# A Mamba and FP4 layer on one core: replicated loads by unit of 32 channels over all partitions

## The chip, the cores and the metric

The kernel runs on one core of a Trainium2 chip. The metric is the device time of one execution in microseconds (us). TensorE multiplies matrices, VectorE, ScalarE and GpSimd work elementwise, SyncE only issues DMAs and waits; 16 DMA engines move data between HBM (DRAM) and the 128 partitions of on-chip memory.

## The reference

The input `x` has 4 sequences of 2048 tokens with 256 features, 8192 tokens in all. It is normalised, goes through four Mamba layers with a residual, and then through a gated feed-forward block whose activations and weights are quantised to FP4 in blocks of 16. The part around the change is the selective scan of each Mamba layer: 512 channels `d`, 16 states `n`:

```
dA = exp(delta[t, d] * A[d, n])
h  = h * dA + (delta[t, d] * u[t, d]) * B[t, n]
y[t, d] = sum over n of h * C[t, n]   (+ u * D_skip, then * silu(z), then the output projection)
```

Each of the 512 x 16 pairs (channel, state) is a recurrence over the tokens of its sequence; `delta` and `delta*u` do not depend on the state, `B` and `C` do not depend on the channel.

## The kernel before

The program has three blocks one after another: `normalise_input`, `mamba_layers` and `fp4_ffn`. The change is in `mamba_layers`. That works through 64 chunks: 4 layers times 16 chunks of T = 512 tokens (four chunks make a sequence). A chunk is a turn of 16 groups (`s` = 0 to 15). A group is one set of 4 states (`j = s % 4`) of one block of 128 channels (`q = s // 4`), and its rows are laid out so: partition 32*k + r holds state 4*j + k of channel 32*unit + r, and the free dimension holds unit 0 to 3 and 512 tokens. So 4 units of 32 channels make the 128 channels, and 4 states stand side by side over the partitions.

For this layout three things have to be copied to each of the four groups of 32 partitions:

- `drep[q % 2]` (128 x 4 x 512): delta of block q, once per k. ScalarE reads it in `exp` (L603) to make `dA`, one group ahead of the scan.
- `durep[q % 2]` (same size): delta*x. VectorE multiplies it with `B_all` in `times_b` (L935) to make `bu`; then `scan` (L950) makes `h`.
- `crep[:, j, :]` (128 x 4 x 512): C of state 4*j + k on partitions 32*k to 32*k + 31. GpSimd multiplies it with `h` in `times_c` (L832).

The sources are three DRAM scratch tensors: `delta_dram` and `du_dram` (512 channels x 512 tokens, stored from `za` by `store_delta` and from `relu` by `store_du`) and `c_dram` (16 states x 512 tokens). They are written and read back in each chunk; both have two halves for alternate chunks. All these DMAs are issued by SyncE, in the order in which `turn` is written, and each may wait for a semaphore first. In turn g the order is: C unit 3 and durep block 1 of this chunk; the stores and loads of x; drep 2, durep 2; the store of the next chunk's C; drep 3, durep 3; the next x; then for the next chunk the stores of delta (`store_delta`, L372) and of delta*x (`store_du`, L376), drep 0, durep 0, C units 0 and 1, drep 1, C unit 2. drep and durep have two buffers each, so the load of block q + 2 waits until all of block q has been read; crep has one buffer per j and waits until the last group of the chunk before has been multiplied.

Before, `replicate` (L348) fills one buffer with four DMAs, one per k: DMA k writes partitions 32*k to 32*k + 31 with all four units, and its source pattern is 32 rows, 4 units, 512 floats. `load_c` (L342) fills crep for one j with four DMAs: each writes 32 partitions with the same row. Each buffer has its own semaphore; a DMA adds 16 when it has landed, so a consumer waits for 64 per load. VectorE waits for durep in front of the first `times_b` of a block, ScalarE for drep in front of the first `exp`, GpSimd for crep in the first four groups of a chunk.

GpSimd also computes delta (`za`) and delta*x (`relu`, L854) for the next chunk during the groups 7 to 11 of this one. The turns run in a hardware loop of four chunks per pass (`turns`).

Of the kernel before, what the change touches and what calls it, by code (L numbers as in the profile page):

```python
# [11 lines left out]
P = 128  # L12
T = 512
# [11 lines left out]
def positive(count):  # L25

    return not isinstance(count, int) or count > 0
# [88 lines left out]
def mamba_layers(nc, xbuf, w, NL, L, sem, x_stored):  # L116
# [17 lines left out]
    with ExitStack() as ctx:  # L134
        def sb(name, shape, dt=F32):
            return ctx.enter_context(nc.sbuf_tensor(name, shape, dt))
# [32 lines left out]
        crep = sb("crep", [P, QS, T])  # L169
# [8 lines left out]
        c_dram = nc.dram_tensor("c_dram", (2, 4 * QS, T), F32, kind="Internal").ap()  # L178
# [12 lines left out]
        c_loaded = [sem(f"c_loaded{j}") for j in range(QS)]  # L191
# [93 lines left out]
        def _(sp):  # L285
# [50 lines left out]
            def load_c(n, p_, j):  # L336
                if positive(n):
                    sp.wait_ge(hc_ready, 2 * (NG * (n - 1) + NG - QS + j) + 2)
                if j == 0:
                    sp.wait_ge(c_stored, 16 * (n + 1))  # L340
                for k in range(4):
                    sp.dma_start(crep[32 * k:32 * k + 32, j, :],  # L342
                                 c_dram[p_, 4 * j + k].partition_broadcast(32)).then_inc(c_loaded[j], 16)

            def replicate(dst, src, q, done):
                rows = src[P * q:P * q + P].rearrange("(g r) t -> r g t", r=32)
                for k in range(4):
                    sp.dma_start(dst[32 * k:32 * k + 32], rows).then_inc(done, 16)  # L348

            def load_delta(n, p_, q):  # L350

                if q >= 2:
                    sp.wait_ge(da_ready, 4 * NG * n + 16 * (q - 2) + 16)
                elif q == 0:
                    sp.wait_ge(delta_stored, 16 * (n + 1))
                elif positive(n):
                    sp.wait_ge(da_ready, 4 * NG * n)
                replicate(drep[q % 2], delta_dram[p_], q, d_loaded[q % 2])

            def load_du(n, p_, q):  # L360

                if q >= 2:
                    sp.wait_ge(bu_ready, 2 * NG * n + 8 * (q - 2) + 8)
                elif q == 0:
                    sp.wait_ge(du_stored, 16 * (n + 1))
                elif positive(n):
                    sp.wait_ge(bu_ready, 2 * NG * n)
                replicate(durep[q % 2], du_dram[p_], q, du_loaded[q % 2])
# [28 lines left out]
            for j in range(QS):  # L397
                load_c(0, 0, j)
# [7 lines left out]
            def turn(g, ph):  # L406
                n, p_ = g + 1, 1 - ph % 2
                if not is_first(g):
                    load_c(g, 1 - p_, 3)
                load_du(g, 1 - p_, 1)  # L410
                if not is_first(g):
                    at_layer(g, ph, lambda layer: load_skip(layer, g))
                    if not (isinstance(g, int) and g == 1):
                        store_x(g - 2)
                    load_res(g - 1, (ph - 1) % 4)
                load_delta(g, 1 - p_, 2)
                load_du(g, 1 - p_, 2)
                if not is_last(g):
                    store_c(n, p_)
                load_delta(g, 1 - p_, 3)  # L420
                load_du(g, 1 - p_, 3)
                if not is_last(g):
                    if not (isinstance(g, int) and g == TOT - 2):
                        at_layer(g + 2, (ph + 2) % 4, lambda layer: load_inw(layer, g + 2))
                        at_layer(g + 2, (ph + 2) % 4, load_mid)
                        load_x(g + 3)
                    store_delta(n, p_)
                    store_du(n, p_)
                    load_delta(n, p_, 0)
                    load_du(n, p_, 0)  # L430
                    load_c(n, p_, 0)
                    load_c(n, p_, 1)
                    load_delta(n, p_, 1)
                    load_c(n, p_, 2)
# [384 lines left out]
        def _(pool):  # L819

            def times_c(at):
                n, s, G = at
                j = s % QS
                if s < QS:
                    pool.wait_ge(c_loaded[j], 64 * (n + 1))
                r = 4 * (s % 2)
                for k in range(2):
                    pool.wait_ge(scanned, 4 * G + 2 * k + 2)
                    if positive(2 * G + k - 3):
                        pool.wait_ge(summed, 2 * G + k - 3)  # L830
                    pair = slice(r + 2 * k, r + 2 * k + 2)
                    pool.tensor_tensor(hc[:, pair, :], h[:, pair, :], crep[:, j:j + 1, :].to_broadcast([P, 2, T]),  # L832
                                       ALU.mult).then_inc(hc_ready, 1)
# [57 lines left out]
            def turn(g, ph):  # L891
                other = 1 - ph % 2
                for s in range(NG):
                    if not is_last(g):
                        if s == 2:
                            silu_xc(g + 1, other)
                        if s == 7:
                            softplus(g + 1, other, 0)
                    times_c(group(g, s))
                    if not is_first(g):  # L900
                        if s == 10:
                            variance(g - 1)
                        if s == 12:
                            newton_step(g - 1)
                    if not is_last(g):
                        if s == 8:
                            softplus(g + 1, other, 1)
                        if s in (10, 11):
                            softplus(g + 1, other, s - 8)
                    if not is_first(g):  # L910
                        if s == 15:
                            affine(g - 1, 0)
                            affine(g - 1, 1)
# [721 lines left out]
```

## Time and profile before

| | |
|---|---|
| time of 3 runs | 8876.08, 8876.52, 8879.55 us; median 8876.52 |
| the profiled execution | 8879.16 us, span in the trace 8877.4 us |
| VectorE busy | 8002.6 us (90%) |
| GpSimd busy | 6905.2 us (78%) |
| TensorE busy | 6565.6 us (74%) |
| ScalarE busy | 5352.6 us (60%) |
| DMA | 910 MB, 42% of the 16 engines' time |

Engines are named PE (TensorE), PEld (its weight loads), DVE (VectorE), ACT (ScalarE), POOL (GpSimd) and SP (SyncE; SPq is its sequencer, which issues the DMAs). L348 is line 348 of the kernel. Times are microseconds from the span's start unless marked ns. Releasers (after `<-`) are inferred from semaphore events.

### The profile page before, as it was taken

The numbers are of one execution on the slowest core, as the hardware profiler recorded it, in microseconds if no ns is written. First come the engines' busy times: TensorE is split into PE (matmuls) and PEld (weight loads), VectorE is DVE, ScalarE is ACT, GpSimd is POOL, SyncE is SP. The second block draws the span as 40 slices with busy tenths as digits, with TensorE's granted clock in tenths as the row PEclk, the third lists the DMA queues.
The fourth block names the chain that finished last, engine by engine and source line by source line (L and its number), as shares of the span: only waits on it lengthen the run. The fifth ranks groups of instructions, "written<-read, shape, count | busy, mean of one in ns | idle before, by whom it ended". The sixth has DMA issues, their size and how long they took to land. (4 is left out here: it accounts for less than half of the span.)

```text
span 8877.4 us, 97211 instructions
## 1 busy us (share of the span) xinstructions
PE 6565.6 (74%) x21284; PEld 2595.9 (29%) x21284; DVE 8002.6 (90%) x8268; ACT 5352.6 (60%) x8662; POOL 6905.2 (78%) x3198
## 2 busy tenths in 40 slices
PE   3777777778777777777777777777777777646656
PEld 1222222222222222222222222222222222224434
DVE  3999999999999999999999999999999999845555
ACT  2666666666666666666666666666666666422222
POOL 1888888888888888888888889888888889732222
PEclk9899998989899999898899989898989999767888
DMA  4444454544444544454445545444445455310000
GB/s 136 105 105 112 115 119 110 119 122 113 106 110 113 119 111 118 112 128 115 99 113 117 119 110 119 122 113 106 110 113 119 112 117 119 71 36 22 24 26 24
DMA packets 568694, 910.48 MB, mean 103 GB/s; under 512 B 58320, under 2 KB 203088, under 8 KB 566992
## 3 DMA queue, kind: packets, MB, share of 16 engines
q1 hardware_dynamic: 568016, 903.29, 42.4%
q8 instruction: 200, 3.28, 0.2%
q14 instruction: 478, 3.92, 0.2%
HBM read 716.41 MB, written 186.65 MB: 102 GB/s over the span
## 5 line engine op out<-in xcount | busy, mean ns | idle before, releaser
L832 POOL TENSOR_TENSOR hc<-h,crep 128x1024 f32<-128x1024 f32 x2048 | 4785.0, 2361 | 834.8 <-PE acc L473 748.6
L950 DVE TENSOR_TENSOR_SCAN h<-dA,carry,bu 128x512 f32<-128x512 f32 x3072 | 3768.2, 1265 | 92.7 <-ACT dA L603 46.7
L935 DVE TENSOR_TENSOR bu<-durep,B_all 128x1024 f32<-128x1024 f32 x2048 | 2483.2, 1212 | 194.6 <-DMA durep<-du_dram 146.1
L603 ACT ACTIVATE dA<-drep,cur 128x512 f32<-128x512 f32 x4096 | 2618.6, 710 | 14.5 <-DMA drep<-delta_dram 14.5
L455 PE MATMUL B_all<-dtc,spread_b 128*128 128x512 f32 x2048 | 1360.6, 752 | 1638.1 <-DVE bu L935 1636.6
L612 ACT COPY carry<-h 128x4 f32<-128x4 f32 x1023 | 200.9, 196 | 2223.5 <-DVE h L950 2168.7
L473 PE MATMUL acc<-hc,gather 128*32 128x512 f32 x8192 | 1281.8, 702 | 5.5 <-POOL hc L832 5.5
L950 DVE TENSOR_TENSOR_SCAN h<-dA,bu 128x512 f32<-128x512 f32 x1024 | 1196.7, 1206 | 9.9 <-ACT dA L603 7.8
L493 PE MATMUL work<-xT,inw 128*128 128x512 f32 x2048 | 1020.6, 644 | 60.5 <-ACT xT L623 50.0
L455 PEld LDWEIGHTS B_all<-dtc,spread_b 128*128 128x128 f32 x2048 | 367.6, 213 | 2321.5 <-DVE bu L935 2258.2
L503 PE MATMUL work<-xs,taps 128*128 128x512 f32 x2048 | 964.1, 614 | 0.0
L493 PEld LDWEIGHTS work<-xT,inw 128*128 128x128 f32 x2048 | 400.5, 207 | 758.9 <-issue 662.1
L1073 POOL TENSOR_TENSOR f_f_qh_xn<-f_hid,f_f_qh_rec 128x704 f32<-128x704 f32 x64 | 101.5, 1585 | 630.7 <-DVE f_f_qh_rec L1068 630.7
L503 PEld LDWEIGHTS work<-xs,taps 128*128 128x128 f32 x2048 | 376.1, 194 | 617.9 <-issue 617.9
L1280 PE MATMUL f_down<-f_wdT,f_hqT 128*128 128x256 f32 (+1 forms) x768 | 259.7, 494 | 341.1 <-ACT f_hqT L1329 341.1
L531 PE MATMUL work<-outw,sz 128*128 128x256 f32 x2048 | 489.6, 382 | 0.0
L473 PEld LDWEIGHTS acc<-hc,gather 128*32 128x32 f32 x8192 | 173.0, 116 | 979.8 <-issue 688.0
L844 POOL TENSOR_TENSOR quad<-quad,xs 128x2048 f32<-128x2048 f32 x64 | 289.4, 4522 | 160.2 <-ACT quad L701 160.2
L531 PEld LDWEIGHTS work<-outw,sz 128*128 128x128 f32 x2048 | 394.4, 193 | 55.6
L837 POOL TENSOR_TENSOR xc<-xc,quad 128x2048 f32<-128x2048 f32 x64 | 289.9, 4530 | 142.0 <-ACT quad L668 142.0
L462 PE MATMUL acc<-xc,skip 128*128 128x512 f32 x512 | 339.4, 752 | 0.0
L1280 PEld LDWEIGHTS f_down<-f_wdT,f_hqT 128*128 128x128 f32 (+1 forms) x768 | 177.4, 246 | 413.1 <-ACT f_hqT L1329 358.6
(167 smaller groups left out, 7151.8 us busy)
## 6 DMA issues: line engine op xcount, KB each, us to landing
drep<-delta_dram SPq DMA_DIRECT2D x1024, 256.0 KB, 6.0
durep<-du_dram SPq DMA_DIRECT2D x1024, 256.0 KB, 6.7
crep<-c_dram SPq DMA_DIRECT2D x1024, 64.0 KB, 6.5
delta_dram<-za SPq DMA_DIRECT2D x64, 1024.0 KB, 4.3
du_dram<-relu SPq DMA_DIRECT2D x64, 1024.0 KB, 5.3
x_in<-xbuf SPq DMA_DIRECT2D x65, 512.0 KB, 3.8
x_res<-xbuf SPq DMA_DIRECT2D x64, 512.0 KB, 3.9
xbuf<-x_res SPq DMA_DIRECT2D x64, 512.0 KB, 5.6
```

What stands on the lines that cost most here:

```text
L455: pe.matmul(B_all[:], spread_b[:, s % QS, :], dtc[:, p_, :], start=True, stop=True).then_inc(bb_ready, 1)
L462: pe.matmul(acc[:], skip[:, q, :], xc[:, p_, q, :], start=True, stop=False, skip_group_check=True)
L473: ins = pe.matmul(acc[32 * k:32 * k + 32, :], gather[:], hc[:, 4 * (s % 2) + k, :], start=False, stop=s % QS == QS - 1, skip_group_check=True)
L493: ins = pe.matmul(W[b][:], inw[:, k, z * DI + e * P:z * DI + (e + 1) * P], xT[:, k, :], start=k == 0, stop=k == KD - 1)
L503: ins = pe.matmul(W[b][:], taps[:, 4 * e + k, :], xs[:, e, k:k + T], start=k == 0, stop=k == 3)
L531: ins = pe.matmul(half, sz[:, p_, k, t * P:(t + 1) * P], outw[:, k, :], start=False, stop=k == DB - 1)
L603: act.activation(dA[:, 4 * (s % 2) + k, :], drep[q % 2][:, k, :], ACT.Exp, scale=cur[:, p_, 4 * s + k:4 * s + k + 1]).then_inc(da_ready, 1)
L832: pool.tensor_tensor(hc[:, pair, :], h[:, pair, :], crep[:, j:j + 1, :].to_broadcast([P, 2, T]), ALU.mult).then_inc(hc_ready, 1)
L837: pool.tensor_tensor(xc[:, p_], xc[:, p_], quad[:], ALU.mult).then_inc(xc_ready, 1)
L935: dve.tensor_tensor(bu[:, 2 * k:2 * k + 2, :], durep[q % 2][:, 2 * k:2 * k + 2, :], B_all[:].unsqueeze(1).to_broadcast([P, 2, T]), ALU.mul ...
L950: dve.tensor_tensor_scan(h[:, r, :], dA[:, r, :], bu[:, k, :], start, ALU.mult, ALU.add).then_inc(scanned, 1)
L1280: ins = pe.matmul(down[:, 0:D], hqT[0:rows, tt % 2, k, :], wdT[0:rows, k, :], start=k == 0, stop=k == GT - 1)
```

## The change

`load_c` and `replicate` are cut the other way. A DMA of `replicate` now takes one unit of 32 channels and writes it to all 128 partitions, that is four times; its source is the 32 rows with a leading level of 4 and step 0. `load_c` takes the four states of one j in one DMA: the source is 4 rows, each repeated 32 times through a step of 0 in the middle. The number of DMAs for drep and durep stays four per block; for C it goes from four to one per j, and GpSimd waits for 16 instead of 64. What stands where in the buffers is the same.

```diff
@@ -338,14 +338,12 @@
                     sp.wait_ge(hc_ready, 2 * (NG * (n - 1) + NG - QS + j) + 2)
                 if j == 0:
                     sp.wait_ge(c_stored, 16 * (n + 1))
-                for k in range(4):
-                    sp.dma_start(crep[32 * k:32 * k + 32, j, :],
-                                 c_dram[p_, 4 * j + k].partition_broadcast(32)).then_inc(c_loaded[j], 16)
+                sp.dma_start(crep[:, j, :], c_dram[p_, 4 * j:4 * j + 4].unsqueeze(1).to_broadcast([4, 32, T])).then_inc(c_loaded[j], 16)
 
             def replicate(dst, src, q, done):
-                rows = src[P * q:P * q + P].rearrange("(g r) t -> r g t", r=32)
-                for k in range(4):
-                    sp.dma_start(dst[32 * k:32 * k + 32], rows).then_inc(done, 16)
+                for unit in range(4):
+                    rows = src[P * q + 32 * unit:P * q + 32 * unit + 32]
+                    sp.dma_start(dst[:, unit, :], rows.unsqueeze(0).to_broadcast([4, 32, T])).then_inc(done, 16)
 
             def load_delta(n, p_, q):
 
@@ -822,7 +820,7 @@
                 n, s, G = at
                 j = s % QS
                 if s < QS:
-                    pool.wait_ge(c_loaded[j], 64 * (n + 1))
+                    pool.wait_ge(c_loaded[j], 16 * (n + 1))
                 r = 4 * (s % 2)
                 for k in range(2):
                     pool.wait_ge(scanned, 4 * G + 2 * k + 2)
```

## Rows read from the trace of the kernel before

**Rows 1.** The page: busy time of each engine, and VectorE's slices.
```profile
PE 6565.6 (74%) x21284; PEld 2595.9 (29%) x21284; DVE 8002.6 (90%) x8268; ACT 5352.6 (60%) x8662; POOL 6905.2 (78%) x3198
DVE  3999999999999999999999999999999999845555
```

**Rows 2.** Waits of VectorE: us in total, times, longest us.
```profile
DVE bu L935 <- DMA durep<-du_dram: 146.1, 38, 99.1
```

**Rows 3.** The page's DMA issues: count, KB each, median us to landing.
```profile
drep<-delta_dram SPq DMA_DIRECT2D x1024, 256.0 KB, 6.0
durep<-du_dram SPq DMA_DIRECT2D x1024, 256.0 KB, 6.7
```

**Rows 4.** Windows: busy us per engine, clock, DMA share, GB/s.
```profile
4070.50:4071.50 1.00, 1.00 (x10) 0.16 (x9) 1.00 (x2) 0.00 (x0) 1.00 (x2) 1.00 1.03 389
4079.50:4080.50 1.00, 1.00 (x4) 0.40 (x3) 1.00 (x2) 0.31 (x2) 1.00 (x2) 1.00 1.01 379
4004.50:4012.00 7.50, 5.63 (x19) 1.89 (x18) 6.96 (x7) 3.39 (x7) 6.60 (x4) 1.00 1.06 210
4034.00:4039.00 5.00, 1.76 (x10) 0.16 (x8) 4.57 (x5) 5.00 (x9) 3.00 (x2) 1.00 1.07 220
4085.00:4091.00 6.00, 5.90 (x23) 1.97 (x26) 6.00 (x7) 3.83 (x8) 6.00 (x4) 1.00 1.06 214
212.00:7740.00 7528.00, 5831.65 (x18746) 2125.39 (x18750) 7329.88 (x6899) 5029.16 (x8062) 6555.18 (x2988) 0.90 0.48 113
```

**Rows 5.** Timeline of SyncE at a chunk boundary: start, us, what, count.
```profile
4077.84 0.36 SPq L376 DMA_DIRECT2D du_dram<-relu  x1
4078.32 3.20 SPq L348 DMA_DIRECT2D drep<-delta_dram  x4
4083.09 1.73 SPq L348 DMA_DIRECT2D durep<-du_dram  x4
4085.01 5.68 SPq L342 DMA_DIRECT2D crep<-c_dram  x8
4090.80 1.78 SPq L348 DMA_DIRECT2D drep<-delta_dram  x4
4093.04 7.72 SPq L342 DMA_DIRECT2D crep<-c_dram  x8
```

**Rows 6.** Timeline: GpSimd's delta*x, VectorE's first product of blocks 0 to 3.
```profile
4073.25 4.56 POOL L854 TENSOR_TENSOR relu<-za,xc 128x2048 f32<-128x2048 f32 x1
...
4094.15 1.23 DVE L935 TENSOR_TENSOR bu<-durep,B_all 128x1024 f32<-128x1024 f32 x1 [2.11 <-DMA durep<-du_dram]
...
4122.91 1.23 DVE L935 TENSOR_TENSOR bu<-durep,B_all 128x1024 f32<-128x1024 f32 x1 [0.31 <-PE B_all L455]
...
4151.36 1.21 DVE L935 TENSOR_TENSOR bu<-durep,B_all 128x1024 f32<-128x1024 f32 x1
...
4181.36 1.23 DVE L935 TENSOR_TENSOR bu<-durep,B_all 128x1024 f32<-128x1024 f32 x1
```

**Rows 7.** The C loads of line 342: ns min/median/max of one issue.
```profile
L342 SPq DMA_DIRECT2D crep<-c_dram x1024: 302/421/1878, 155.0 to 7635.3; - x171
```

**Rows 8.** Timeline of ScalarE and VectorE where the four-chunk loop turns.
```profile
4209.78 1.21 DVE L935 TENSOR_TENSOR bu<-durep,B_all 128x1024 f32<-128x1024 f32 x1
...
4215.19 0.20 ACT L612 COPY carry<-h 128x4 f32<-128x4 f32 x1 [6.62 <-issue]
...
4218.63 1.28 DVE L950 TENSOR_TENSOR_SCAN h<-dA,carry,bu 128x512 f32<-128x512 f32 x1 [6.47 <-ACT dA L603]
...
4245.61 1.23 DVE L935 TENSOR_TENSOR bu<-durep,B_all 128x1024 f32<-128x1024 f32 x1 [0.49 <-PE B_all L455]
```

**Rows 9.** Timeline of the very start of the Mamba part.
```profile
190.13 3.64 SPq L348 DMA_DIRECT2D drep<-delta_dram  x8
...
193.81 0.43 SPq L376 DMA_DIRECT2D du_dram<-relu  x1
...
204.50 1.73 SPq L348 DMA_DIRECT2D durep<-du_dram  x4
...
211.34 1.23 DVE L935 TENSOR_TENSOR bu<-durep,B_all 128x1024 f32<-128x1024 f32 x1 [99.11 <-DMA durep<-du_dram]
```

## The prediction

> **What bounds the kernel now.** I read the page's busy shares and slices first [rows 1], then who waits for whom on VectorE [rows 2], then the DMA issues and the rate of the transfers by stretch [rows 3, 4], and last the order of time at one chunk boundary [rows 5, 6]. The page says that VectorE is busy in over 90% of nearly every slice up to the 33rd, where the Mamba part ends; in the stretch from 212 to 7740 us it works 7330 of 7528 us [rows 4]. GpSimd is behind it with 6555 us. So the 64 chunks follow VectorE, at about 117.7 us each (first product of the first chunk at 211.3 us, of the one read here at 4094.2, 33 chunks later [rows 6, 9]).
>
> VectorE's only sizeable wait on a transfer is 146.1 us for durep, in 38 places, 99.1 of it at the very start [rows 2]; the other 47 us are 0.75 us per chunk boundary. That small number is the important one: it says that the first durep load of a chunk lands just when it is needed, with no reserve. The chain at a boundary [rows 5, 6]: GpSimd finishes delta*x at 4077.8 us, SyncE stores it, issues drep for block 0 behind it (4078.3), durep for block 0 at 4083.1, and VectorE starts the chunk at 4094.2 after 2.1 us of waiting.
>
> **The rates.** I call "a block" the four DMAs that fill one drep or durep buffer: 4 x 256 KB = 1.05 MB [rows 3]. In stretches that hold only such loads the 16 DMA engines are all busy (share 1.06) and move 210, 220 and 214 GB/s; in stretches that hold only a store of all 128 partitions they are as busy (1.03, 1.01) and move 389 and 379 GB/s [rows 4]. So an engine moves 24.0 GB/s when it writes or reads alone and 13.4 GB/s in the replicating loads. Those write 32 partitions per DMA with 16 engines; the factor 1.8 says that the way into 32 partitions carries eight engines' worth. A block now takes b = 1.05 MB / 214 = 4.9 us.
>
> **The change, part by part.**
>
> Issues. The C load goes from 16 to 4 issues per chunk, 768 fewer in all, at 0.42 us each [rows 7]: 323 us of SyncE, which computes nothing and mostly waits in this kernel. At the boundary the C loads stand behind the first durep in SyncE's order [rows 5], so nothing on the path moves forward: I take 0. The ends are -323 us, if every issue stood on the path, and, since a three-level issue has no row of its own, 2304 issues times the 1.46 us between the median and the longest one, which SyncE's idle time would mostly hide; both ends are far from the nearest row, a SyncE that waits between the blocks [rows 5]. The wait for one completion instead of four costs nothing. drep and durep keep their four issues per block; their bytes, and their places in the buffers, stay too.
>
> Shape. Each new DMA writes all 128 partitions, which takes the factor 1.8 away if all 16 engines work on it. But its source is now a three-level pattern: 4 copies with step 0, then 32 rows, then 512 floats. The destination is 128 rows. No transfer in the trace has an outermost level below 16, and none shows how such a one is dealt out. Two ends: all 16 engines, 384 GB/s, b = 2.7 us; or, if the engines get equal shares of the outermost level, four shares on four engines. Four at 24.0 GB/s give 96 GB/s and b = 10.9 us; four at the slower 13.4 give 53.6 and b = 19.6 us. The second slows again because engine 0 would fill partitions 0 to 31 while engine 1 fills 32 to 63, and so on; if such neighbours meet on the same way into the memory as the engines of a 32-partition DMA do today, each gets half. I take four engines: dealing out the outermost level is what fits every full-rate row (128 or 32 rows over 16 engines), and a level of 4 can't be cut further. Between 10.9 and 19.6 I take b = 12.0: only two engines meet on eight ways, not sixteen, and they meet only when both are at the same four-or-so rows, so I allow a tenth.
>
> The Trainium skill, page "DMA: Bandwidth & Descriptors", section "Why a DMA increments its semaphore by 16 and not by 1", says that the number of engines is the largest up to 16 that divides the slowest non-1 dimension of both patterns, and its rules for kernel authors name a leading zero-stride broadcast of c copies as confined to at most c engines; by this rule b lies at 10.9 or above, and no run so far shows it. The page "SBUF — State Buffer", section "Door 1: The DMA port swizzle", speaks against the neighbours: partitions p and p+32 are on the same port, and 64 partitions reach no more ports than 32. The 214 against 384 GB/s agrees with it; by it alone four engines in step would be at 19.6.
>
> Where b falls on the path, per chunk (a C load is b/4, in the same queue):
>
> 1. Chunk start. From delta*x ready to durep landed are now 16.3 us: the store (1.05 MB / 384 = 2.7), drep (4.9), durep (4.9), and 3.8 of issue and landing. It becomes 16.3 + 2(b - 4.9). As the reserve is nil, all of it is stall: 14.2 us at b = 12.0. Nothing earlier can hide it: drep block 0 waits for the delta store, but is issued after the delta*x store in SyncE's order. What is queued behind VectorE's wait is every scan.
>
> 2. Block 1. After the first durep, in order: C units 0 and 1, drep 1, C units 2 and 3, durep 1: b/4 x 4 + 2b = 3b after the start of the chunk. VectorE asks for durep 1 after block 0: 28.8 us in the chunk of [rows 6] (4094.15 to 4122.91), and 35.8 us (4209.78 to 4245.61) in every fourth chunk, where ScalarE stands still 6.6 us at the edge of the four-chunk loop and VectorE behind it [rows 8]; that is 49 and 14 chunks. 3b is 14.7 now and hidden; at b = 12.0 it is 36.0: a stall of 7.2 us in 49 chunks and 0.2 in 14.
>
> 3. Blocks 2 and 3. The x stores and loads come first (3 us), then 2b = 24.0: 27.0 against the 28.4 that block 1 takes (4122.91 to 4151.36 [rows 6]): hidden, with little over. Block 3 has 24.0 against 30.0 (to 4181.36): hidden.
>
> 4. The very start. drep 0, drep 1 and durep 0 stand in a row before the first product [rows 9]: 3(b - 4.9) = 21 us.
>
> Sum at b = 12.0: 63 x 14.2 + 49 x 7.2 + 14 x 0.2 + 21 = 895 + 353 + 3 + 21 = 1272 us. On the profiled execution (span 8877.4, its own time 8879.2, which is 2.7 above the median of 8876.5) that is a span of 10,149; the median follows at **10,150 us**. By the same steps b = 10.9 gives 756 + 191 + 18 = 965, about 9,840. b = 13.5 gives 1084 + 573 + 66 + 26, and block 2 then asks 30.0 where 28.4 are to be had, 1.6 x 63 = 101: 1,850, about 10,730. The FP4 part behind 7790 us has none of these loads and stays.
>
> **The rivals.**
>
> A. The neighbours share fully, b towards 19.6. For it: the same engines do get half today [rows 4]. Against: today eight ways are loaded by sixteen engines at all times, there two engines walk over eight ways. Price at b = 19.6: start 63 x 29.4 = 1852; block 1 (58.8 - 28.8) x 49 + 23 x 14 = 1792; block 2 (3 + 39.2 - 28.4) x 63 = 869; block 3 (39.2 - 30) x 63 = 580; 44 at the very start: 5137, so 14,010 us. In that case the four engines are the bound (9 blocks x 19.6 = 176 us per chunk and the stores beside it). Half way, b = 15: 1273 + 794 + 129 + 290 + 30 = 2516, 11,390 us.
>
> B. All 16 engines are used, b = 2.7, and the kernel is faster. What decides it is the dealing out alone, at any count of engines that gives b below 4.9 (nine or more at 24 GB/s). It takes away the 47 us at the boundaries and 3 x 2.2 at the start: 8,823 us. For it: destination rows are 128, as in the fast stores; more than that is not to be had, since VectorE's own work is 97% of the stretch. Against: the zero-step level of 4 on the outside.
>
> C. Four engines, but the stall is hidden by something I take for serial, no change within 0.2% (18 us, about what a measurement of this kernel can tell from nothing). Against: the 0.75 us of wait per boundary leaves no reserve for even one block.
>
> **How the numbers follow.** Four engines with b from 10.9 to 13.5: 0.50, the likeliest, own range 9,800 to 10,750. Slower sharing up to 19.6 or beyond: 0.40, of which 0.10 above 13,200. B: 0.08. C: 0.02. So faster 0.08, same 0.02, slower 0.90. The range 9,700 to 13,200 leaves out B, C and the top of A.
>
> **What would show it.** Right: the mean DMA share in loading stretches falls from 1.06 to about 0.25 at some 90 GB/s; VectorE's wait for durep grows from 146 to some 1,400 us with two waits per chunk, about 14 at block 0 and 7 at block 1; the landing of a drep or durep DMA grows from 6 us to over 12; the C issues fall to 256. If b is larger, the wait shows at blocks 2 and 3 as well, and the chunk nears 9b plus some 20 us. Wrong: a share near 1.0 at 380 GB/s in those stretches and no wait for durep after the first (B). If the share is 0.25 and the time still below 9,700, then the sum of the path is wrong, most likely in that block 1 is asked for later than I read.

## The result and the profile after

The changed kernel takes **9838.8 us** (median of 4 runs, 9836.5 to 9840.8) against 8876.3 us before (4 runs on the same chip): ratio 1.109, 95% interval 1.107 to 1.111, slower by 962 us. The profiled execution has a span of 9839.0 us. The forecast was 10,150 us, slower, in a range of 9,700 to 13,200.

The page of the changed kernel shows the same work at a lower share: VectorE is busy for 8011 us as before (8003), but most slices of the Mamba part are at 8 tenths, where nearly all were at 9 in [rows 1]. The DMA queue moves the same 903 MB in 25.4% of the engines' time instead of 42.4%.

```profile
PE 6660.9 (68%) x21284; PEld 2616.6 (27%) x21284; DVE 8010.9 (81%) x8268; ACT 5350.4 (54%) x8662; POOL 6907.7 (70%) x3198
DVE  3898888888888889888888988888888888865555
q1 hardware_dynamic: 528080, 903.13, 25.4%
crep<-c_dram SPq DMA_DIRECT2D x256, 256.0 KB
```

In the windows of the changed kernel (columns as in [rows 4]; the DMA share and GB/s are the last two), the first two stretches hold only the new loads and the third only a store of 128 partitions:

```profile
4008.00:4020.00 12.00, 11.14 (x34) 3.23 (x33) 11.97 (x15) 5.26 (x10) 12.00 (x6) 0.89 0.26 98
4056.00:4080.00 24.00, 9.87 (x28) 2.81 (x30) 11.10 (x11) 6.50 (x12) 11.78 (x6) 0.69 0.26 98
4039.00:4039.60 0.60, 0.60 (x5) 0.30 (x2) 0.60 (x1) 0.00 (x0) 0.60 (x1) 1.00 1.03 382
```

Share 0.26 of sixteen is four engines, at 98 / 4 = 24.5 GB/s each: the full rate of an engine working alone (389 / 16 = 24.3 in [rows 4]). A block of 1.05 MB takes 10.7 us instead of 4.9. The order of time at one boundary, SyncE and GpSimd first, then VectorE's first product of blocks 0, 1 and 2; it answers to [rows 5, 6]:

```profile
4040.79 4.56 POOL L852 TENSOR_TENSOR relu<-za,xc 128x2048 f32<-128x2048 f32 x1
...
4045.37 0.37 SPq L374 DMA_DIRECT2D du_dram<-relu  x1
4045.87 3.54 SPq L346 DMA_DIRECT2D drep<-delta_dram  x4
4050.69 10.12 SPq L346 DMA_DIRECT2D durep<-du_dram  x4
4061.02 5.06 SPq L341 DMA_DIRECT2D crep<-c_dram  x2
4066.20 10.52 SPq L346 DMA_DIRECT2D drep<-delta_dram  x4
4076.85 5.98 SPq L341 DMA_DIRECT2D crep<-c_dram  x2
4082.96 10.33 SPq L346 DMA_DIRECT2D durep<-du_dram  x4
...
4072.47 1.23 DVE L933 TENSOR_TENSOR bu<-durep,B_all 128x1024 f32<-128x1024 f32 x1 [12.90 <-DMA durep<-du_dram]
...
4105.44 1.23 DVE L933 TENSOR_TENSOR bu<-durep,B_all 128x1024 f32<-128x1024 f32 x1 [4.43 <-DMA durep<-du_dram]
...
4133.88 1.21 DVE L933 TENSOR_TENSOR bu<-durep,B_all 128x1024 f32<-128x1024 f32 x1
```

GpSimd has delta*x ready at 4045.3; VectorE begins the chunk 27.1 us later (16.3 before), after 12.9 us of waiting, waits another 4.4 us for block 1 at 33.0 us, and not for block 2. The issues show the queue too: four durep DMAs took 1.7 us to issue in [rows 5] and take 10.1 here. That SyncE is held until the queue has room is my reading of it. Who VectorE waited for, in the changed kernel (us in total, times, longest):

```profile
DVE bu L933 <- DMA durep<-du_dram: 1106.9, 131, 121.2
DVE bu L933 <- PE B_all L453: 68.9, 55, 14.7
DVE h L948 <- issue: 53.8, 14, 3.9
```

The durep wait grew by 1106.9 - 146.1 = 961 us [rows 2], as much as the whole loss of 962; other waits moved too, and nearly cancel. Added up over the trace by block: 739 us more in front of block 0 and 205 more in front of block 1 in chunks 1 to 63 (waits of the product for TensorE at those two places counted in), 8 for blocks 2 and 3, 22 at the very start, and 34 less in the scans; the remaining 22 us are spread. ScalarE now waits 347 us for drep (14.5 before), but VectorE waits for durep, which lands after it.

One more load chain grew behind the new loads. The store of x (`xbuf<-x_res`) stands behind durep 1 in SyncE's order, SyncE waits for its landing before it loads the next x, and drep 2 comes after that. The row of its landing on the page before and after, and SyncE's wait for it before and after:

```profile
xbuf<-x_res SPq DMA_DIRECT2D x64, 512.0 KB, 5.6
xbuf<-x_res SPq DMA_DIRECT2D x64, 512.0 KB, 12.9
SPq L381 <- DMA xbuf<-x_res: 325.1, 63, 6.1
SPq L379 <- DMA xbuf<-x_res: 653.2, 63, 11.8
```

### The profile page after: what moved, and what is told of

The parts are those of the page before. It is cut to its first block and busy times, and to the rows that moved or that the text cites. A ratio compares the mean times of both kernels' runs of the same rounds, so it can differ in the third digit from the quotient of the medians.

```text
span 9839.0 us, 96443 instructions
## 1 busy us (share of the span) xinstructions
PE 6660.9 (68%) x21284; PEld 2616.6 (27%) x21284; DVE 8010.9 (81%) x8268; ACT 5350.4 (54%) x8662; POOL 6907.7 (70%) x3198
## 3 DMA queue, kind: packets, MB, share of 16 engines
q1 hardware_dynamic: 528080, 903.13, 25.4%
## 5 line engine op out<-in xcount | busy, mean ns | idle before, releaser
L933 DVE TENSOR_TENSOR bu<-durep,B_all 128x1024 f32<-128x1024 f32 x2048 | 2488.5, 1215 | 1182.6 <-DMA durep<-du_dram 1106.9
L453 PE MATMUL B_all<-dtc,spread_b 128*128 128x512 f32 x2048 | 1388.6, 766 | 2450.5 <-DVE bu L933 2447.8
L471 PE MATMUL acc<-hc,gather 128*32 128x512 f32 x8192 | 1312.1, 717 | 5.5 <-POOL hc L830 5.5
L501 PE MATMUL work<-xs,taps 128*128 128x512 f32 x2048 | 987.4, 626 | 0.0
L460 PE MATMUL acc<-xc,skip 128*128 128x512 f32 x512 | 339.0, 751 | 34.9 <-DMA skip<-in_skip 34.9
L852 POOL TENSOR_TENSOR relu<-za,xc 128x2048 f32<-128x2048 f32 x64 | 290.6, 4541 | 0.1
## 6 DMA issues: line engine op xcount, KB each, us to landing
xbuf<-x_res SPq DMA_DIRECT2D x64, 512.0 KB, 12.9
```

Source lines behind the costliest of these rows:

```text
L453: pe.matmul(B_all[:], spread_b[:, s % QS, :], dtc[:, p_, :], start=True, stop=True).then_inc(bb_ready, 1)
L460: pe.matmul(acc[:], skip[:, q, :], xc[:, p_, q, :], start=True, stop=False, skip_group_check=True)
L471: ins = pe.matmul(acc[32 * k:32 * k + 32, :], gather[:], hc[:, 4 * (s % 2) + k, :], start=False, stop=s % QS == QS - 1, skip_group_check=True)
L501: ins = pe.matmul(W[b][:], taps[:, 4 * e + k, :], xs[:, e, k:k + T], start=k == 0, stop=k == 3)
L852: pool.tensor_tensor(relu[:], za[:], xc[:, p_], ALU.mult).then_inc(du_ready, 1)
L933: dve.tensor_tensor(bu[:, 2 * k:2 * k + 2, :], durep[q % 2][:, 2 * k:2 * k + 2, :], B_all[:].unsqueeze(1).to_broadcast([P, 2, T]), ALU.mul ...
```

## The experiments

Theory F is the prediction's: a DMA whose source has an outermost level of 4 entries runs on four engines, and the time follows from the order of the loads. The experiments take it at the full rate of each engine, as the windows above show it, and for 2 entries as well. All ratios are to the kernel before on the same chip.

### c_only: only the C loads changed

```diff
-                for k in range(4):
-                    sp.dma_start(crep[32 * k:32 * k + 32, j, :],
-                                 c_dram[p_, 4 * j + k].partition_broadcast(32)).then_inc(c_loaded[j], 16)
+                sp.dma_start(crep[:, j, :], c_dram[p_, 4 * j:4 * j + 4].unsqueeze(1).to_broadcast([4, 32, T])).then_inc(c_loaded[j], 16)
```

with 16 instead of 64 in GpSimd's wait.

> Only the C loads are changed (one DMA per j, source level of 4 outermost); drep and durep load as before. Theory F (a DMA with an outermost level of 4 runs on four engines at 24 GB/s each, and the time follows from the order of the loads): a C unit takes 2.7 us instead of 1.2, durep 1 lands 2 x 4.9 + 4 x 2.7 = 20.6 us after the chunk's start and is asked for after 28.8, so the stall does not come: 8,876 us, within 18. Theory S (the C loads are what costs, since GpSimd waits for a C unit on one slow DMA): over 9,000 us. DMA issues of C 256.

Measured: 8913.6 us (5 runs), ratio 1.0043 (1.0029 to 1.0057): 36 us slower. Theory S is out. The stall before block 0 is what it was, but F's "same" was missed too. VectorE's waits for scan inputs grew:

```profile
DVE bu L933 <- DMA durep<-du_dram: 137.2, 36, 99.8
DVE h L948 <- ACT dA L601: 105.9, 29, 7.3
DVE bu L933 <- PE B_all L453: 82.7, 86, 5.9
```

Before these are 146.1, 54.5 (and 38.9 more as "issue"), and 45.0. Two places were found. Where the four-chunk loop turns, ScalarE stands still longer; this is the answer to the ScalarE row of [rows 8]:

```profile
4241.36 0.20 ACT L610 COPY carry<-h 128x4 f32<-128x4 f32 x1 [8.62 <-issue]
```

ScalarE lost 121.6 us there in 14 passes (8.7 each) against 52.9 + 38.9 us, 6.6 each, by the same view before, partly booked to VectorE. VectorE hardly feels the difference, though: its waits for scan inputs are 105.9 us against 93.4, 12 more and not 30. And at the three layer changes TensorE waits for `skip` behind the C units (9.4 us in all, none before), with VectorE 5 to 6 us late each time, 16 us together. The loop of twelve, below, tests the first.

### rep_only: only drep and durep changed

The edit is the `replicate` part of the change alone; the C loads and their wait are as before.

> Only drep and durep are changed; C loads as before, four DMAs per j. Theory F: the start of each chunk is late by the full 12 us (durep 0 behind drep 0 on four engines), but durep 1 now lands 2 x 10.9 + 4 x 1.2 = 26.6 us after the start, before the 28.8 at which it is asked for. So the second stall goes, 3 to 4 us in 49 chunks: 8,876 + 63 x 12 + 18 = 9,650 us, 190 less than with both edits. Theory S: near 8,876 us. A theory by which the loss is in proportion to the bytes on the four engines (9 blocks before, 8 now): 9,730 us.

Measured: 9709.0 us (4 runs), ratio 1.094 (1.092 to 1.096). So nearly all the loss, 831 of 962 us, is the two replicated buffers. By block: 846 us of waiting before block 0, and only 48 before block 1, where the changed kernel has 234 (29 in the kernel before): the second stall is there only because the C units also stand in the four engines' queue. That part came as forecast, 186 us less. But before block 0 it waits 60 us more than the changed kernel does, 0.9 per chunk. In both, durep 0 is issued 5.3 us after delta*x is ready; VectorE's product follows 28.6 us after it in `rep_only` and 27.8 in the changed kernel (means of 60 chunks). The 0.9 lies in the transfers, and its cause is open. So the two kernels are 130 us apart and not 190. By its time alone (9,709) this run would fit the theory of bytes (9,730) better than F (9,650); what speaks for F is where the waiting is. Bytes in proportion would have left both stalls at eight ninths, but VectorE's waits for durep are now one per chunk:

```profile
DVE bu L935 <- DMA durep<-du_dram: 965.6, 64, 119.1
```

These are 64 waits, against 131 in the changed kernel.

### pairs: two copies per DMA

```diff
                 for unit in range(4):
                     rows = src[P * q + 32 * unit:P * q + 32 * unit + 32]
-                    sp.dma_start(dst[:, unit, :], rows.unsqueeze(0).to_broadcast([4, 32, T])).then_inc(done, 16)
+                    for half in range(2):
+                        sp.dma_start(dst[64 * half:64 * half + 64, unit, :],
+                                     rows.unsqueeze(0).to_broadcast([2, 32, T])).then_inc(done, 16)
```

with 128 instead of 64 in the two waits.

> As the changed kernel, but each DMA of drep and durep is cut in two, each with two copies onto 64 partitions: outermost level 2 instead of 4, 8 DMAs per block. Theory F: two engines, 48 GB/s, b = 21.8 us; start 63 x 33.8, block 1 25.7 and 18.7 us late, block 2 18.2, block 3 13.6, in all about 14,600 us; DMA share 0.13 in loading stretches. Theory N (the chip deals by rows or bytes, and four is an accident of another limit, such as the reads of one row by four copies): the same b as in the changed kernel, 9,840 us. If the rate per engine also falls because engines 0 and 1 fill partitions of the same group of ways: above 20,000 us.

Measured: 14,479.6 us (2 runs), ratio 1.631 (1.628 to 1.634). The forecast by F was 14,600. A window with only these loads, and VectorE's first product of the four blocks of one chunk:

```profile
3895.00:3925.00 30.00, 11.57 (x37) 3.66 (x35) 8.45 (x8) 4.82 (x10) 7.01 (x3) 0.74 0.13 50
```

```profile
3933.68 1.23 DVE L935 TENSOR_TENSOR bu<-durep,B_all 128x1024 f32<-128x1024 f32 x1 [30.23 <-DMA durep<-du_dram]
3987.17 1.23 DVE L935 TENSOR_TENSOR bu<-durep,B_all 128x1024 f32<-128x1024 f32 x1 [23.85 <-DMA durep<-du_dram]
4036.30 1.23 DVE L935 TENSOR_TENSOR bu<-durep,B_all 128x1024 f32<-128x1024 f32 x1 [20.60 <-DMA durep<-du_dram]
4079.50 1.23 DVE L935 TENSOR_TENSOR bu<-durep,B_all 128x1024 f32<-128x1024 f32 x1 [13.12 <-DMA durep<-du_dram]
```

Share 0.13 is two engines, again at 25 GB/s each, so the neighbours cost nothing here either. There are four stalls per chunk, 30.2, 25.0, 20.3 and 13.7 us in the mean, near the expected 33.8, 25.7, 18.2 and 13.6. Theory N is out. In the patterns tried, the outermost count goes with the number of engines: 32 with 16, 4 with 4, 2 with 2.

### inner: the copies' level moved inside

```diff
-                    sp.dma_start(dst[:, unit, :], rows.unsqueeze(0).to_broadcast([4, 32, T])).then_inc(done, 16)
+                    sp.dma_start(dst[:, unit, :], rows.unsqueeze(1).to_broadcast([32, 4, T])).then_inc(done, 16)
...
-                sp.dma_start(crep[:, j, :], c_dram[p_, 4 * j:4 * j + 4].unsqueeze(1).to_broadcast([4, 32, T])).then_inc(c_loaded[j], 16)
+                sp.dma_start(crep[:, j, :], c_dram[p_, 4 * j:4 * j + 4].unsqueeze(0).to_broadcast([32, 4, T])).then_inc(c_loaded[j], 16)
...
-    by_state = w("A_log").reshape(NL, DB, 4, 32, NS // 4, 4).transpose(5, 3, 0, 1, 4, 2).reshape(P, NL, -1)
+    by_state = w("A_log").reshape(NL, DB, 4, 32, NS // 4, 4).transpose(3, 5, 0, 1, 4, 2).reshape(P, NL, -1)
...
-    spread = np.zeros((P, NS // 4, 4, 32), np.float32)
+    spread = np.zeros((P, NS // 4, 32, 4), np.float32)
...
-            spread[R + 4 * j + k, j, k] = 1
+            spread[R + 4 * j + k, j, :, k] = 1
...
-        "gather": np.tile(np.eye(32, dtype=np.float32), (4, 1)),
+        "gather": np.repeat(np.eye(32, dtype=np.float32), 4, axis=0),
```

> The copies' level is moved inside: partition 4*r + k instead of 32*k + r (channel outside, state inside), the same bytes, the same number of DMAs as in the changed kernel, only host-side layouts of A, the B spread and the gather matrix follow. Source of drep and durep: 32 rows, 4 copies with step 0, 512 floats; of C: 32 copies with step 0, 4 rows, 512 floats. Theory F: 16 engines and all 128 partitions, 384 GB/s, b = 2.7 us; the 47 us of waiting at the chunk boundaries and 3 x 2.2 at the start go: 8,823 us, DMA share near 1.0 at 380 GB/s. Theory Z (a source level of step 0 is slow wherever it stands): 9,800 us or more. Theory O (16 engines, but still the slow rate of the 32-partition loads, 214 GB/s): 8,876 us, same.

Measured: 8772.1 us (4 runs), ratio 0.988 (0.9865 to 0.990): 105 us faster than before, 1067 faster than the changed kernel with the same number of DMAs and the same bytes. Theories Z and O are out. The loads now run on all engines over all partitions. The first window holds the delta*x store and then drep, durep and C loads; the second, inside it, holds only drep and durep loads. VectorE's waits follow:

```profile
4026.00:4036.00 10.00, 8.38 (x25) 3.03 (x25) 10.00 (x10) 6.26 (x13) 9.69 (x10) 1.00 0.97 332
4030.50:4033.00 2.50, 2.40 (x12) 0.83 (x12) 2.50 (x4) 2.21 (x5) 2.34 (x4) 1.00 1.05 398
```

```profile
DVE bu L933 <- DMA durep<-du_dram: 98.6, 1, 98.6
DVE bu L933 <- PE B_all L453: 73.2, 95, 4.0
DVE h L948 <- ACT dA L601: 14.9, 20, 1.8
```

The loads alone move 398 GB/s, as fast as the stores (389 and 379), so a block takes 2.6 us; the 332 of the longer window are a mean over faster and slower parts. Only the very first wait for durep is left, as F said. But 54 us were expected and 105 came. The rest is at the standstill where the loop turns: the scans' waits of 54.5 + 38.9 us in the kernel before (for `dA` and "issue") are 14.9 here, 78 less. The products wait 28 us more for TensorE (45.0 before, 73.2 here), which leaves some 50.

### early_after, early_before, early_inner: drep 0 ahead of the delta*x store

```diff
+                    sp.wait_ge(da_ready, 4 * NG * g + 48)
                     store_delta(n, p_)
+                    load_delta(n, p_, 0)
                     store_du(n, p_)
-                    load_delta(n, p_, 0)
```

applied to the changed kernel, the kernel before, and `inner`.

> As the changed kernel, but drep 0 of the next chunk is issued right after the delta store (with a wait for ScalarE's block 2, which frees the buffer), ahead of the delta*x store. The chunk's start had 27.8 us from delta*x ready to durep 0 landed, of them 10.9 for drep 0 on the four engines. Theory F (one queue on four engines, the path of the prediction): drep 0 can start 4 to 5 us before delta*x is ready, when the delta store has landed, so 5 to 6 us of it leave the path; the rest still stands in front of the store's share on those engines: 9,838 - 63 x 5.8 = 9,470 us. If drep 0 left the path altogether: 9,150 us. If the start is set by something else than this queue: 9,840.

Measured: 9706.0 us (4 runs), ratio 1.0934 (1.0915 to 1.095): 133 us less than the changed kernel, not 365. SyncE in one boundary, and VectorE's first product:

```profile
4094.80 0.37 SPq L370 DMA_DIRECT2D delta_dram<-za  x1
4099.16 2.37 SPq L346 DMA_DIRECT2D drep<-delta_dram  x4
4103.87 0.36 SPq L374 DMA_DIRECT2D du_dram<-relu  x1
4115.02 2.37 SPq L346 DMA_DIRECT2D durep<-du_dram  x4
...
4129.86 1.23 DVE L934 TENSOR_TENSOR bu<-durep,B_all 128x1024 f32<-128x1024 f32 x1 [9.78 <-DMA durep<-du_dram]
```

The store (4103.9) stands behind drep 0 on the four engines and has landed only at 4115.0, 11.2 us later; only then may durep be issued. In the changed kernel the store landed in 5.3 us, and durep was queued while drep 0 was still moving. The path changed from store, drep, durep in one unbroken queue to rest of drep, store, landing, durep: less of drep 0 on the path, but a landing more, in which the four engines have nothing. My expectation took the queue as never empty; it left out that durep may be issued only when the store has landed. VectorE's first product comes 25.5 us after delta*x, in the mean, where the expectation has 22.0 and the changed kernel 27.8.

> The kernel before with the same earlier issue of drep 0. At b = 4.9 drep 0 lands about when delta*x is ready, so durep 0 lands about 11.5 us after it instead of 16.3, and VectorE asks after 14 to 15: the 0.75 us per boundary go, 47 us: 8,830 us. If the extra gain of the kernel with the copies inside (8,772 against the 8,823 expected) came from the lighter traffic at the edge of the four-chunk loop, this kernel does not get it, since its transfers take as long; if that gain too came from the start of the chunk, this kernel is near 8,780.

Measured: 8779.3 us (4 runs), ratio 0.988 (0.987 to 0.990): 103 us faster than before, where 47 were expected. The waits for durep went as forecast, and more did:

```profile
DVE bu L936 <- DMA durep<-du_dram: 100.5, 1, 100.5
DVE h L951 <- ACT dA L604: 45.8, 28, 3.2
DVE h L951 <- issue: 4.1, 1, 4.1
```

The scans' waits (54.5 + 38.9 before) are 49.9, the longest 4.1 instead of 6.7 us. So my reading that only lighter transfers could shorten the standstill was wrong. That the old loads, issued 5 us earlier, are out of the way when the loop turns is an argument, and no run isolates it.

> The copies' level inside and drep 0 early. With b = 2.7 no product of VectorE waits for durep after the first any more, so an earlier drep 0 has nothing to take away: 8,772 us, within 15. If the ScalarE side (its wait for drep 0 one group before the chunk's start) still costs, 8,750 or less.

Measured: 8760.6 us (4 runs, 8759.3 to 8764.2), ratio 0.987 (0.985 to 0.988). Over `inner` that is 11 us, within the 15 allowed; the two were not timed side by side, so it is not a difference I would claim.

### before_12, c_only_12, early_inner_12: twelve chunks per pass of the loop

```diff
-            with eng.Fori(0, (TOT - 4) // 4) as i:
-                for r in range(2, 6):
-                    turn(4 * i + r, r % 4)
+            with eng.Fori(0, (TOT - 4) // 12) as i:
+                for r in range(2, 14):
+                    turn(12 * i + r, r % 4)
```

> The kernel before, with twelve chunks per pass of the hardware loop instead of four: 4 edges between passes instead of 14, nothing else. Theory E (at each edge ScalarE stands still 6.6 us until its next instructions are there, and VectorE behind it): 10 x 6.6 = 66 us less, 8,815 us. Rival (the standstill comes with the chunk, for instance its transfers, and not with the edge): 8,880 us.

Measured: 8836.9 us (5 runs), ratio 0.9954 (0.994 to 0.997): 40 us faster, of 66 expected. The standstill goes with the edge: VectorE's share of it is now 4 waits of up to 6.9 us, and ScalarE's "issue" waits are 2 instead of 8 in number, so the rival is out.

```profile
DVE h L950 <- issue: 27.3, 4, 6.9
DVE h L950 <- ACT dA L603: 10.0, 16, 2.1
```

The scans' two waits fell by 54.5 + 38.9 - 37.3 = 56 us, and the products' wait for TensorE rose by 16, which leaves the 40. So of the 66 us 56 went, and 16 came back as another wait.

> The kernel with only the C loads changed, in the loop of twelve. It was 37 us slower than before, where none were expected; ScalarE's standstill at the edges grew from 6.6 to 8.7 us (14 x 2.1 = 30). Theory E: with 4 edges the loss falls to 4 x 2.1 and the 6 us of the three layer changes, about 15 us over the before kernel with the loop of twelve. Rival (the C loads cost something in every chunk, 0.6 us): again 37 us over it.

Measured: 8855.4 us (7 runs), ratio 0.9971 (0.996 to 0.998): 18 us over `before_12` (15 expected), where with the loop of four it was 36. So half of the C loads' price went with the longer loop, as theory E forecast, and the rest fits the three layer changes, where a chunk is 5 us longer with the C edit in both loops. But the traces do not show the half that went at the edges. From first product to first product a chunk at an edge takes 123.3 us in the kernel before and 123.9 in `c_only`, 7 us in 14 passes. An ordinary chunk takes 116.2 us before, 116.6 in `c_only`, and 116.6 in both kernels with the loop of twelve: that is another 15 us in 43 chunks, and its cause is open.

> Copies' level inside, drep 0 early, loop of twelve: the best of all if the parts add. The edge costs this kernel only 1 to 2 us in VectorE's time (block 0 takes 30.0 to 30.6 us there and 29.3 in other chunks), so 10 edges less bring 10 to 20 us: 8,745 us. If the edge costs it as much as it costs the kernel before: 8,695.

Measured: 8764.6 us (4 runs, 8748.1 to 8771.3), ratio 0.987 (0.986 to 0.989), the same as `early_inner` (8760.6) within their spread. Both forecasts, 8,745 and 8,695, were missed. With drep 0 early and b = 2.7 the edge costs so little that fewer edges bring nothing that can be measured. `inner` and `early_inner` are the kernels to keep; they can't be told apart.

## Why the prediction was right

**Reading of the bound, no reserve at the chunk's start.** Right. VectorE's wait for durep grew by as much as the kernel lost (961 and 962 us; the other waits happen to cancel), and `inner` removes that wait where b is made small.

**Four engines.** Right, and shown from both sides: shares of 0.26 and 0.13 with outermost levels of 4 and 2, and 1.05 with 32. The Trainium skill's rule (page "DMA: Bandwidth & Descriptors", section "Why a DMA increments its semaphore by 16 and not by 1") gives 4, 2 and 16 here; the traces agree at all three.

**The size of b.** This is the term that was mis-sized. I allowed a tenth for neighbours that fill partitions 32 apart and took b = 12.0; it is 10.7, nothing was lost to them. The sum of 1272 us becomes 731 + 162 + 17 = 910 at b = 10.7, against 962 measured. So this term put the forecast 362 us too high, and the steps of the path together 52 too low. That the same steps at b = 10.9, written down as the lower end, gave 9,840 us where 9,838.8 was measured is luck: the b of that sum is a little too large, by about what the path lacks. The Trainium skill, page "SBUF — State Buffer", section "Door 1: The DMA port swizzle", gives partitions 0 to 31 half of the ports and puts p and p+32 on the same one. The 214 against 389 GB/s of the old 32-partition loads agrees. But two or four engines walking over such partitions lost nothing here: 98 GB/s on four, 50 on two. Rival A is out.

**The path.** Step 1 (block 0): 2(b - 4.9) = 11.6 us at b = 10.7, 739 us in all over 63 chunks, 11.7 each. Step 2 (block 1): with b = 10.7 the 3b are 32.1 and the stall 3.3 us in 49 chunks, 162 us; 205 were measured. Of the missing part 31 us are at the three layer changes, where the load of `skip` waits behind durep 1 on the four engines; TensorE stood 34.9 us for it. That step I had not priced. Another 8 us are at the loop's edges, where I took the block as too long for a stall. Step 3: hidden, as said, but block 2 by about 1 us, where the step gives 4 at b = 10.7 (3 + 21.4 against 28.4); in some chunks it waits, 8 us more in all. The step took 3 us for the x stores and loads, but the x store lands only after 12.9 us behind durep 1 (5.6 before), and drep 2 is issued behind that, 1.8 us after block 1 has begun. Block 3 has 9 us to spare. `pairs` shows both turn into stalls, of 20.3 and 13.7 us, when b doubles. Step 4: 22 us against 17 at b = 10.7. Against these stand 34 us that the scans gained at the loop's edge (3.8 us of waiting per pass where there were 6.1), which the prediction did not foresee.

**The issues.** 768 fewer C issues brought nothing that can be seen, as forecast. The C edit is not free: it costs 36 us alone, and 130 on top of the other edit, where its transfers stand before durep 1 on the four engines.

**Rival B** (all 16 engines) is not what the change does; `inner` is that case. Its price was too low, 54 us where 105 were gained, mostly because it left out the standstill at the loop's edge.

## What to carry to other kernels

Read a DMA's pattern from the outside: a leading copy level of step 0 with a count of 4 or 2 put the whole transfer on four or two engines here, though it filled 128 or 64 partitions. Put the copies inside the rows (and change the partition order and the small constant matrices to fit). Check it in the windows by the DMA share of a stretch that holds only this load: 0.26 at 98 GB/s against 1.05 at 398.

When a load chain has no reserve at one point (a small wait, repeated at every pass), every change of its transfer time counts once for each transfer in the chain there, and the price can be worked out from the order of issues: 14,600 forecast and 14,480 measured for `pairs`. Count the landings as well, where an issue waits for a store: `early_after` was forecast to gain 365 us without one, and gained 133.

## What the runs showed that was not expected

At the edge of the hardware loop ScalarE stands still with nothing to wait for, and how long differs with the order and form of the loads: 6.6 us per pass before, 8.7 with the C units on four engines; VectorE's longest wait there is 6.7 us before, 4.1 with drep 0 issued 5 us earlier, 1.8 with the copies' level inside. `before_12` shows that the standstill comes with the edge. That the next instructions come over the same DMA engines, and are late when those are loaded, is my reading; the profile's page lists instruction packets among the DMA queues, but no run isolated it.

A store placed behind a long load on the same few engines lands late: the delta*x store took 11.2 us instead of 5.3 in `early_after`, which gave back most of what issuing the load early had gained, and the x store took 12.9 us instead of 5.6 in the changed kernel.
